# Shared down tiles begun ahead of the last silu, and the S4 sums spread over VectorE and GpSimd

## What is computed

```python
xt = x.reshape(T, H)                                    # after a layer norm
probs = softmax(xt @ w_router); topk_p, topk_idx = top_k(probs, 4)
gate = (xt @ w_gate).reshape(T, K, I); up = (xt @ w_up).reshape(T, K, I)
basis = silu(gate) * up
mixed = einsum('tek,tki->tei', mix[topk_idx], basis)
out = einsum('teh,te->th', einsum('tei,ih->teh', mixed, w_down), coeff)
shared = silu(xt @ shared_w_gate) * (xt @ shared_w_up) @ shared_w_down
x = x + tanh(g_ffn) * (out + shared)
```

## Time and profile before

| | us |
|---|---|
| median of 3 runs | 981.62 (979.45 to 984.07) |
| the profiled execution | 981.09 |
| its span, first to last instruction | 979.2 |
| TensorE busy | 911.4 (93%) |
| VectorE busy | 568.9 (58%) |
| GpSimd busy | 477.6 (49%) |
| ScalarE busy | 408.4 (42%) |

### The profile page before, as it was taken

The page is one execution under the profiler, slowest core; times in us unless marked ns, Lnnn a source line. Parts: engine busy times, 40 slices in busy tenths (PEclk is TensorE's granted clock), DMA queues, the critical chain, the costliest instruction groups (busy, mean ns, idle before and its releaser), DMA issues.

```text
span 979.2 us, 17727 instructions
## 1 busy us (share of the span) xinstructions
PE 911.4 (93%) x6744; PEld 778.0 (79%) x6744; DVE 568.9 (58%) x1123; ACT 408.4 (42%) x858; POOL 477.6 (49%) x525
## 2 busy tenths in 40 slices
PE   6869999999998999989998979889999999999998
PEld 6768989888888979777786857678888888888886
DVE  5447575766667574666223654855556565555657
ACT  4655444453535353454311423333444444344431
POOL 1123061513333150325122997726688887888841
PEclk9979999999999999999999989999999999999999
DMA  6695567474747464697010113441110201201026
GB/s 222 169 189 156 128 165 194 136 198 118 200 131 203 108 190 112 159 254 250 1 44 22 43 52 124 139 161 44 66 65 28 81 22 65 86 22 66 22 95 249
DMA packets 80422, 117.01 MB, mean 120 GB/s; under 512 B 6345, under 2 KB 49098, under 8 KB 79306
## 3 DMA queue, kind: packets, MB, share of 16 engines
q1 hardware_dynamic: 78592, 115.11, 41.3%
q10 hardware_dynamic: 1746, 0.77, 0.4%
HBM read 77.13 MB, written 37.81 MB: 117 GB/s over the span
## 4 chain that ended last, share of the span: by engine, by line
PE 75%; DVE 9%; POOL 6%; DMA 4%; issue 4%; ACT 2%; SPq 1%; ACTq 0%; DVEq 0%; POOLq 0%
PE ps_proj L1550 21%; PE ps_scores L1849 18%; PE ps_scoresT L1849 9%; PE ps_o L1661 5%; PE ps_scores L1629 4%; PE ps_proj L1849 4%; PE ps_scoresT L1648 4%; PE ps_scores L1550 3%; PE ps_scoresT L1550 2%; DMA q_stack<-max_rows 2%; DVE actT_lo L1185 2%; DVE neg_max L1220 2%; DVE o_blocks L1238 1%; DMA q_kept<-qT_hi 1%; PE ps_o L1550 1%
## 5 line engine op out<-in xcount | busy, mean ns | idle before, releaser
L1220 DVE TENSOR_REDUCE neg_max<-ps_scores 128x2 f32<-128x384 f32 (+1 forms) x256 | 128.8, 513 | 139.0 <-PE ps_scores L1629 137.1
L910 ACT ACTIVATE probsT<-ps_scoresT 128x512 f32<-128x512 f32 (+1 forms) x256 | 134.9, 542 | 144.7 <-PE ps_scoresT L1648 141.3
L1629 PE MATMUL ps_scores<-k_stack,q_stack 114*128 114x192 f32 (+1 forms) x512 | 105.4, 290 | 13.9 <-DVE neg_max L1220 9.2
L1108 ACT ACTIVATE part_sums<-ps_scores 128x512 f32<-128x512 f32 x96 | 57.4, 598 | 137.9 <-PE ps_scores L1849 137.9
L1648 PE MATMUL ps_scoresT<-q_stack,k_stack 116*128 116x256 f32 x448 | 104.2, 304 | 6.7 <-DMA q_stack<-max_rows 4.6
L1629 PEld LDWEIGHTS ps_scores<-k_stack,q_stack 114*128 114x128 f32 x512 | 81.0, 195 | 27.8 <-DVE neg_max L1220 17.9
L673 POOL TENSOR_TENSOR o_normal<-o_blocks,inv_sums 128x128 f32<-128x128 f32 x64 | 25.7, 402 | 147.0 <-DVE inv_sums L1240 147.0
L796 POOL TENSOR_TENSOR w_expert_lo<-w_sums,w_expert_hi 128x256 fp32r<-128x256 f32 x64 | 64.2, 1015 | 45.8 <-ACT w_expert_hi L1039 45.8
L808 POOL TENSOR_TENSOR big<-big,basis 128x512 f32<-128x512 f32 x56 | 77.5, 1401 | 14.9 <-DVE basis L1494 14.9
L1648 PEld LDWEIGHTS ps_scoresT<-q_stack,k_stack 116*128 116x128 f32 x448 | 71.6, 194 | 9.8 <-DMA q_stack<-max_rows 5.2
L679 POOL TENSOR_TENSOR oT_lo<-oT_raw,oT_hi 128x256 fp32r<-128x256 f32 x32 | 23.5, 736 | 111.2 <-ACT oT_hi L919 111.2
(11 more groups left out here) (262 smaller groups left out, 2549.3 us busy)
## 6 DMA issues: line engine op xcount, KB each, us to landing
k_stack<-k_kept SPq DMA_DIRECT2D x64, 192.0 KB, 5.5
q_stack<-q_kept SPq DMA_DIRECT2D x31, 384.0 KB, 5.4
q_kept<-qT_hi SPq DMA_DIRECT2D x16, 512.0 KB
big<-coeff_rows SPq DMA_DIRECT2D x8, 1024.0 KB, 4.7
xn_rows<-in_x SPq DMA_DIRECT2D x8, 512.0 KB, 4.5
k_kept<-kT_hi SPq DMA_DIRECT2D x16, 256.0 KB
q_kept<-qT_lo SPq DMA_DIRECT2D x8, 512.0 KB
x_rows<-in_x SPq DMA_DIRECT2D x8, 512.0 KB, 5.4
```

The source lines that it names most:

```text
L910: act.activation(PT[:, g % 2, 2 * j:2 * j + blocks].rearrange("p h f r w -> p (h f r w)"), ST[:, n % 2, 0:blocks].rearrange("p h n -> p (h ...
L1108: act.activation(TP[:, u % 2, j, :], src[:, u % 2, :], ACT.Copy).then_inc(taken, 1)
L1220: dve.tensor_reduce(NM[:, g % 2, 2 * i:2 * i + 2], SA[:, n % 2, :, 0:keys], AX.X, ALU.max, negate=True).then_inc(max_done, 1)
L1629: ins = pe.matmul(SA[:, n % 2, f, 0:2 * (near.stop - near.start)], QS[0:TOP, g, i, f].rearrange("p r w -> p (r w)"), keys[:, near, :].rear ...
```

## The change

- ScalarE makes the high parts of down tiles 0 and 1 ahead of silu 15, and VectorE their low parts ahead of the last product.
- The high parts of s3 and s2 of block 3 move from silu 14 to t = 2 of the down loop.
- The seven high copies of expert block 0's weights, all at t = 5 before, are cut into four at t = 5 and three at t = 6.
- S4 of blocks 0 and 1 stays on VectorE, one operation behind each of tiles 8 to 13. S4 of blocks 2 and 3 moves from VectorE (unit 0) to GpSimd, behind `total(3)` and behind the last low s1; its last operation waits for the S4 sums ahead of it.
- The high parts of S4 move to t = 11 and 14 and behind the loop, the low parts to t = 12 and 15 and behind it; unit 0 has none of them left.

```diff
--- before.py
+++ after.py
@@ -62,8 +62,9 @@
 TILE_ORDER = tuple(2 * p + j for p in PAIR_ORDER for j in range(2))
 EARLY = 5
 W_ORDER = (B11, B21, T1, T2, T3, B22, T4)
-SUMS_AT = {8: 0, 10: 1, 12: 2, 14: 3}
+SUMS_AT = {8: 0, 10: 1, 12: 2}
 S1_AT = {3: 0, 7: 1, 10: 2, 13: 3}
+S4_BY_DVE, S4_OP = 2, {8 + m: divmod(m, 3) for m in range(6)}
 
 
 SUMS = [("s3", 0), ("s2", 0), ("s3", 1), ("s2", 1), ("s3", 2), ("s2", 2), ("s3", 3), ("s2", 3)]
@@ -778,6 +779,18 @@
             link(pool.tensor_tensor(s1, s1, v("a21", "lo"), ALU.add))
             pool.tensor_tensor(s1, s1, v("a22", "lo"), ALU.add).then_inc(s_raw, 1)
 
+        def sum4(i):
+
+
+            c, g = BLOCKS[i]
+            v = lambda name, h: operand(name, h, c, g).bitcast(F32)
+            dst = two(TP[:, i // 2, i % 2, :])
+            pool.wait_ge(c_mm, NG)
+            link(pool.tensor_tensor(dst, v("a12", "hi"), v("s2", "hi"), ALU.subtract))
+            link(pool.tensor_tensor(dst, dst, v("a12", "lo"), ALU.add))
+            pool.wait_ge(s4_raw, i)
+            pool.tensor_tensor(dst, dst, v("s2", "lo"), ALU.subtract).then_inc(s4_raw, 1)
+
         def weight_sums(n):
             pool.wait_ge(raw_in[(EXPERT + n) % 2], (EXPERT + n - (EXPERT + n) % 2) * 16 + 32)
             if n >= 1:
@@ -838,7 +851,9 @@
         weight_sums(1)
         sum_low("s1", 2)
         total(3)
+        sum4(2)
         sum_low("s1", 3)
+        sum4(3)
         for u in range(UNITS_E):
             n, g = divmod(u, 2)
             if n < LAST:
@@ -1038,8 +1053,18 @@
                     act.wait_ge(t_sums, n + 1)
                 act.activation(WS[n % 2]["hi"][:, w, :], w_source(n, w), ACT.Copy).then_inc(e_hi, 1)
 
+        def shared_hi(t):
+
+            act.wait_ge(prod_done, (NS - 1) * NG + t // TILES + 1)
+            if t >= 2:
+                act.wait_ge(sd_mm, t - 1)
+            act.activation(DL["hi"][:, t % 2], at_tile(hT, t), ACT.Copy).then_inc(sd_hi, 1)
+
         used = {(n, t): q for q, (n, t) in enumerate(TILES_S)}
         for q in range(FIRST_TILES, len(TILES_S)):
+            if q == len(TILES_S) - 1:
+                shared_hi(0)
+                shared_hi(1)
             silu(q)
             if q == 7:
                 split_hi(SHARED + 2, (up_mm, used[0, 3] + 1))
@@ -1056,13 +1081,6 @@
             if q == 11:
                 split_hi(SDOWN + 1)
 
-        def shared_hi(t):
-
-            act.wait_ge(prod_done, (NS - 1) * NG + t // TILES + 1)
-            if t >= 2:
-                act.wait_ge(sd_mm, t - 1)
-            act.activation(DL["hi"][:, t % 2], at_tile(hT, t), ACT.Copy).then_inc(sd_hi, 1)
-
         def coeff_columns(q):
             act.wait_ge(coeff_t, q + 1)
             act.activation(coeffT[:, group_columns(q)], PC[q % 2], ACT.Copy).then_inc(coeff_out, 1)
@@ -1073,7 +1091,8 @@
             act.activation(cS[:, group_columns(q)], PC[q % 2][0:KB], ACT.Copy).then_inc(c_out, 1)
 
         for t in range(NT):
-            shared_hi(t)
+            if t >= 2:
+                shared_hi(t)
             if 1 <= t <= NG:
                 coeff_columns(t - 1)
             elif NG < t <= 2 * NG:
@@ -1081,14 +1100,21 @@
             if t == 2 * NG + 1:
                 act.wait_ge(c_out, NG)
                 act.dma_start(c_rows, cS).then_inc(c_kept, 16)
+            if t == 2:
+                sum_high("s3", len(BLOCKS) - 1)
+                sum_high("s2", len(BLOCKS) - 1)
             if t in S1_AT:
                 sum_high("s1", S1_AT[t])
             if t == 5:
                 act.wait_ge(raw_in[EXPERT % 2], (EXPERT - EXPERT % 2) * 16 + 32)
                 act.wait_ge(up_mm, NS * NG)
-                weight_high(0, W_ORDER)
-            if t in (10, 12):
-                sum4_high((t - 10) // 2)
+                weight_high(0, W_ORDER[:4])
+            if t == 6:
+                weight_high(0, W_ORDER[4:])
+            if t in (11, 14):
+                sum4_high((t - 11) // 3)
+        for i in range(S4_BY_DVE, len(BLOCKS)):
+            sum4_high(i)
 
         def pair_hi(i):
 
@@ -1122,10 +1148,7 @@
             else:
                 act.wait_ge(s4_lo, 2 * (u + 1))
             take(u, 1, PG, 0)
-            if u == 0:
-                sum4_high(2)
-                sum4_high(3)
-            else:
+            if u >= 1:
                 second_silu(u - 1)
             if n < LAST:
                 if u == 0:
@@ -1395,22 +1418,25 @@
             elif step == 12:
                 dve.tensor_tensor(probs, probs, over(w["top_inv"][:]), ALU.mult).then_inc(coeff_done, 1)
 
+        def shared_lo(t):
+
+            dve.wait_ge(sd_hi, t + 1)
+            dve.tensor_tensor(DL["lo"][:, t % 2], at_tile(hT, t), DL["hi"][:, t % 2].bitcast(F32),
+                              ALU.subtract).then_inc(sd_lo, 1)
+
         mixture()
         steps = {7: (0,), 8: (1,), 9: (4, 5), 10: (6, 7), 11: (8,), 12: (9,), 13: (10, 11), 14: (12,)}
         for q in range(FIRST_TILES, len(TILES_S)):
             if q == FIRST_TILES + 1:
                 for m in range(NG):
                     logits_rows(m)
+            if q == len(TILES_S) - 1:
+                shared_lo(0)
+                shared_lo(1)
             shared_times(q)
             for step in steps.get(q, ()):
                 top_experts(step)
 
-        def shared_lo(t):
-
-            dve.wait_ge(sd_hi, t + 1)
-            dve.tensor_tensor(DL["lo"][:, t % 2], at_tile(hT, t), DL["hi"][:, t % 2].bitcast(F32),
-                              ALU.subtract).then_inc(sd_lo, 1)
-
         def add_rows(i, rows, src, mm, done):
 
             dve.wait_ge(mm, i + 1)
@@ -1421,18 +1447,21 @@
             dve.wait_ge(xb_in[t % 4], 16 * (t // 4 + 1))
             add_rows(t, XB[t % 4], PJ[:, t % 2, :], sd_mm, sd_out)
 
-        def sum4(i):
+        def sum4(i, step):
 
 
             c, g = BLOCKS[i]
+            v = lambda name, h: operand(name, h, c, g).bitcast(F32)
             dst = two(TP[:, i // 2, i % 2, :])
-            if i == 0:
-                dve.wait_ge(c_mm, NG)
-                dve.wait_ge(s_lo, 2 * len(BLOCKS))
-            link(dve.tensor_tensor(dst, operand("a12", "hi", c, g).bitcast(F32), operand("s2", "hi", c, g).bitcast(F32),
-                                   ALU.subtract))
-            link(dve.tensor_tensor(dst, dst, operand("a12", "lo", c, g).bitcast(F32), ALU.add))
-            dve.tensor_tensor(dst, dst, operand("s2", "lo", c, g).bitcast(F32), ALU.subtract).then_inc(s4_raw, 1)
+            if step == 0:
+                if i == 0:
+                    dve.wait_ge(c_mm, NG)
+                    dve.wait_ge(s_lo, 2 * len(BLOCKS))
+                link(dve.tensor_tensor(dst, v("a12", "hi"), v("s2", "hi"), ALU.subtract))
+            elif step == 1:
+                link(dve.tensor_tensor(dst, dst, v("a12", "lo"), ALU.add))
+            else:
+                dve.tensor_tensor(dst, dst, v("s2", "lo"), ALU.subtract).then_inc(s4_raw, 1)
 
         def sum4_low(i):
             c, g = BLOCKS[i]
@@ -1445,13 +1474,14 @@
         for t in range(NT):
             if t >= 2:
                 add_shared(t - 2)
-            shared_lo(t)
-            if t in (9, 11):
-                sum4((t - 9) // 2)
-            if t in (13, 14):
-                sum4_low(t - 13)
+                shared_lo(t)
+            if t in S4_OP:
+                sum4(*S4_OP[t])
+            if t in (12, 15):
+                sum4_low((t - 12) // 3)
         for t in range(NT - 2, NT):
             add_shared(t)
+            sum4_low(S4_BY_DVE + t - (NT - 2))
 
         def gate_first(u):
             dve.wait_ge(taken, 3 * u + 1)
@@ -1505,16 +1535,10 @@
                               ALU.subtract).then_inc(d_lo, 1)
 
         for u in range(UNITS_E):
-            if u == 0:
-                sum4(2)
-                sum4(3)
-            else:
+            if u >= 1:
                 up_second(u - 1)
                 times_up(u - 1, 0)
             gate_first(u)
-            if u == 0:
-                sum4_low(2)
-                sum4_low(3)
             if u >= 1:
                 basis(u - 1, 0)
                 up_first(u - 1)
```

## The result

| | us |
|---|---|
| changed kernel, median of 7 runs | 972.96 (969.84 to 976.71) |
| before, median of 7 runs | 980.95 |
| ratio | 0.9923, 95% interval 0.9898 to 0.9948 |
| profiled execution, its span | 969.84, 968.0 |

The kernel is 0.8% faster. The profiled execution is the fastest of the seven, 3.1 us under their median; before, the profiled one lay at the median.

What follows compares the result with a forecast made beforehand. TensorE's gaps and slow clock between 570 and 652 us were the loss; GpSimd's and TensorE's chains meet level at T2, moving T3 from 653.9 to 641.9 to 645.3, 10.5 us less: 971.0, range 965.5 to 977.5 (8 in 10).

Steps and rivals of the forecast that it cites:

- The first gap: Ahead of the first down tile: TensorE's gap of 6.60 us and its 2.73 us of slow clock go.
- GpSimd's price: Down loop, t = 2: the moved sums cost GpSimd 1.2 us, and total(0) ends at 593.1.
- the gap ahead of tile 4: TensorE ahead of down tile 4: a new gap of some 3.5 us, as ScalarE's sum_high waits for GpSimd's total(0).
- The clock behind it: Behind the new gap at tile 4: a clock loss between 1.9 and 2.7 us, taken as 2.3.
- The weight copies: Expert 0's seven copies on ScalarE, ahead of shared_hi(6): cut into 4 and 3, the 0.52 us gap goes.
- S4 on VectorE: Tiles 8 to 13: gaps of 1.84 and 0.70 us become 0.3 to 0.6 at each tile, 2 to 4 us.
- rival B: Tiles 8 to 13: VectorE becomes the bound, 4.2 us a tile; 3 to 6 us less, 975 to 978; chance 0.18.
- S4 on GpSimd: Six operations join GpSimd's queue, taken as 9 us; the 2.47 us gap and its 1.9 of slow clock go.
- The sum: At T2 of unit 0 GpSimd's and TensorE's chains are level; 8.6 to 12.0 us less, taken as 10.5.
- The ceiling: Shared down tiles to T3 of unit 0: at most about 20 us to be had, 12.1 of gaps, the rest clock.
- half paid back: The new gap ahead of tile 4 and its clock loss give back half of the 6.60 us first gap.
- Rival D: Tiles 8 to 13: gaps of 1.5 us or more put TensorE at 1.2 GHz; 6 us more, 987; chance 0.04.

Runs made afterwards that it cites:

- s1 one tile later: Changed kernel with the high part of s1 block 0 at t = 4 in place of 3; median 970.77 us, ratio 0.9896 to the kernel before.
- second set of runs: The changed kernel unaltered, run again beside the kernel before on the same chip; median 971.82 us, ratio 0.9908.
- the early tiles: Kernel before with only early down tiles 0 and 1 and the moved sums of block 3; median 979.54 us, ratio 0.9987.
- the S4 edits: Kernel before with only the S4 edits, first gap and weight copies as before; median 976.46 us, ratio 0.9956.
- the early tiles with s1 later: Kernel before with early down tiles, moved sums of block 3 and the high part of s1 block 0 at t = 4; median 971.10 us, ratio 0.9902.
- S4 on VectorE alone: Changed kernel with s1 block 0's high part at t = 4 and GpSimd's S4 sums on VectorE around the last additions; median 969.55 us, ratio 0.9893.

## Why the prediction was right, point by point

**The first gap.** Right to the tenth: 578.02, full pace. The two low parts took 3.46 us beside GpSimd, where 1.2 to 2.2 were forecast, and tile 0's was still in time; in two of the other profiles it came 0.2 us late.

**GpSimd's price and the gap ahead of tile 4.** Right in place, cause and size: GpSimd waits 1.30 us for the moved sums, `total(0)` ends at 593.0 (forecast 593.1), TensorE resumes at 595.07 (595.1) behind 3.25 us (3.5). **The clock behind it** was charged 2.3 us flat. It is an event that came in five of the six profiles with that gap: 0 in the first one, 2.5 in the next (5.49 less 3.02). Here the sum against one execution went astray from the median.

**The weight copies.** The 0.52 gap goes with the cut and comes back without it; with s1 one tile later 0.45 us stand there again, though the copies are cut.

**S4 on VectorE.** This step failed in part. VectorE's additions follow each other by 3.0 to 3.4 us in these tiles (by 5.0 where the fourth operation stands), the top of what was said: beside GpSimd a single sum cost up to 1.78, as rival B had it, while the low part took 0.7 to 1.4. The argument against B, "only back to back operations showed 1.7", misread the rows. The highest of the low parts in the earlier trace rows, 1776 ns, is a single one, with VectorE idle ahead of it:

```profile
602.26 1.78 DVE L1411 TENSOR_TENSOR down_lo<-big,down_hi 128x512 fp32r<-128x512 f32 x1 [0.65 <-ACT down_hi L1064]
```

And the step named six tiles with gaps of 0.3 to 0.6 us, "too short for the clock to fall", but left out what its own list of edits has at t = 12: a low part of S4 as a fourth operation, which gave 2.06 us ahead of tile 13, and in some executions a fallen clock. Moving it took the gap away. The eight tiles from 8 to 15 took 4.7 us more than 21.8, where 2 to 4 were forecast. In the profiled execution this miss and the clock that did not fall (2.3 us) cancel; the forecast T3 of 641.9 to 645.3 was met at 642.77 with two errors in it, which is luck. (The upper end is itself 0.5 us too high: with eight tiles by 3.4 us T2 comes at 642.1, not 642.6.)

**S4 on GpSimd.** Six operations took 9.6 us (forecast 8.0 to 10.1, taken 9), the last ended at 637.75 (637.9), T2 started at 640.05 (639.1 to 641). That both chains are level is shown by the kernel with s1 later: 3.25 us less of idle time for TensorE ahead of tile 4, 0.9 less in the stage.

**The sum.** 10.5 less was forecast for the profiled execution, its stage has 10.5 and its span 11.2. The median fell by 8.0 (981.0 to 973.0), and by 9.1 in the second set of runs. 971.0 was forecast, 972.96 and 971.82 were measured. The mis-sized terms are the clock, charged 2.3 us flat, which cost nothing in one profile and 4.0 us in the next (2.5 behind tile 4, 1.5 behind tile 13), and the pause of 2.06 us ahead of tile 13. How often each fall comes in the runs without a profile is not shown.

**The ceiling** of 20 us was too high. Stage less gaps is 64.8 - 7.1 = 57.7 us, where I had 634 - 578.6 = 55.4. A tile behind a pause takes 2.98 to 3.03 us against 2.73, and one behind the small products of tiles 4 to 7 takes 2.95. The first goes with the pauses, some 1 us, the second doesn't. So I estimate that 18 to 19 us were there to be had; the shortest stage measured, 62.2, has 13.1 of them.

**What was not in the prediction at all** is how little the parts add up. By medians the early tiles give 1.4 us, the S4 edits 4.4, both with the cut copies 9.1, the early tiles with s1 later 9.5, and the changed kernel with s1 later 10.1. The early tiles hold most of the gain, but only once the wait that they uncover is moved; with it moved, the S4 edits are worth no more than can be measured. The forecast said "half paid back"; by the medians it was nearly all of it, 8.4 us between the two kernels with the early tiles alone. The profiles account for 6.8 of these (73.0 to 66.2). The rest, 1.6, is less than the 2.3 us by which the first of the two profiles lies under its median; no profile shows where the middling run loses them.

## What to carry to other kernels

When an engine's work is moved forward, list every wait that its programs meet at their new times: here ScalarE came to GpSimd's `total(0)` 9 us earlier than before and 3.75 us ahead of its end. With the early tiles alone, moving one copy a tile later was worth as much as the whole change; in the changed kernel it was worth 1 us, within the intervals. Count each tile's operations on the second busiest engine, rare ones too, and price those with two SBUF operands at what they cost beside the other engine. And where a gap is long enough to lower TensorE's clock in some executions, compare medians, not profiles, and compare the granted clock of two profiles, stretch by stretch, before their spans.

## What the runs showed of the hardware

In this stage, gaps of 1.84 to 3.3 us lowered TensorE's clock to 0.50 in some executions and not in others, of the same kernel too (at tile 4, 3.25: no, 3.23: yes; at tile 13, 2.06: no, 2.05: yes), for a loss of 1.5 to 2.5 us each time; those of 0.83 us and less never did. Rival D had a point between 0.70 and 1.84 us from which the clock falls. The length alone gives no such point: it fell behind 1.84 (before) and 2.29 (early tiles only), and not behind 2.39 (S4 on VectorE alone). Outside the stage it also fell within 2 us behind a gap of 1.47 us (at 450 us, before and in the first profile of the changed kernel), and in the second profile of the changed kernel it did not.

A VectorE subtraction of 128 x 512 with both inputs in SBUF took 0.68 us with GpSimd at rest and up to 1.78 beside it, and GpSimd's went from 1.27 to 1.6 or 1.7; VectorE's additions that read PSUM kept their 0.75 us. The Trainium skill (SBUF — State Buffer, "SBUF: two separate sides") has the port pair that the two engines share held for a whole instruction by the one that starts first. By that rule an operation that arrives just behind GpSimd's would take 0.68 + 1.27 = 1.95 us, an estimate from the two times alone; the trace's 1.77 and 1.78 are near that, and the lock itself is not shown.
